# A cross-attention pipeline: where three key chunks are scaled, transposed and evicted

## Chip, core and metric

The kernel runs on one core of a Trainium2 chip. The metric is the time of one execution on the device, in microseconds (us), of which the median of several runs is taken. The engines are named as in the profile: PE is TensorE's matmul stream and PEld its weight loads, DVE is VectorE, ACT is ScalarE, POOL is GpSimd, SP is SyncE, which issues most DMAs.

## What is computed

A decoder layer on x of 16 batches x 100 tokens x 512, in three parts: causal self-attention with 16 heads, cross-attention to a context of 361 tokens per batch, and a feed-forward layer that routes each token to 2 of 8 experts; a layer norm follows each. The change lies in the cross-attention, which has 16 query heads of 128 and 4 key/value heads, so that four query heads share one key head:

```python
q = (hidden_states @ Wq + bq).reshape(b, s, NH, HD).transpose(0, 2, 1, 3)
k = (encoder_hidden_states @ Wk + bk).reshape(b, se, NKV, HD).transpose(0, 2, 1, 3)
v = (encoder_hidden_states @ Wv + bv).reshape(b, se, NKV, HD).transpose(0, 2, 1, 3)
k = jnp.repeat(k, GROUPS, axis=1)
v = jnp.repeat(v, GROUPS, axis=1)
q = _rmsnorm(q, qn_w)
k = _rmsnorm(k, kn_w)
scores = jnp.einsum('bhsd,bhed->bhse', q, k) * scale
scores = scores + attention_mask[:, None, :, :]
probs = jax.nn.softmax(scores.astype(jnp.float32), axis=-1).astype(q.dtype)
out = jnp.einsum('bhse,bhed->bhsd', probs, v)
out = out.transpose(0, 2, 1, 3).reshape(b, s, NH * HD)
return out @ Wo
```

## The kernel before

Self-attention runs first and leaves the queries of the cross-attention in memory; the feed-forward part comes last. `cross_attention_phase` takes the 16 batches one after the other. Its program is written by hand, one instruction list for each engine, and semaphores join the lists: an engine runs its own list strictly in the order written. Batches 0 and 1 are written out, batches 2 to 13 are a loop of six turns with two batches in each, and batches 14 and 15 and a rest are written out again (`over_batches`).

A batch j has four quarters s = 0 to 3, one for each key head. Every product that needs more than a single reduced-precision pass is made of three matmuls, from a high and a low part of both factors (`product3`, line 70). So whatever comes out of a matmul and goes into another is evicted from its PSUM bank twice: ScalarE writes the high part ("hi"), VectorE the low part ("lo", bank minus high part).

In quarter s, TensorE makes the scores of four heads (`scores`); between them it transposes the probabilities of the quarter before (`transpose_probs`, line 855), three chunks of 121 keys, and puts output products in (`output`). Then comes the values product of the quarter before (`values_product`, nine matmuls into `o_bank`). VectorE masks each head's scores and takes their minimum (`masked`, line 1117), ScalarE exponentiates (`exponent`, line 1014), VectorE inverts the sums in two pairs (`invert_sums`, line 1123), and GpSimd multiplies the four heads by them (`normalise`, lines 1253 and 1278). The values product is evicted by ScalarE to oTh (line 1052) and by VectorE to oTl (line 1181).

The keys of the next batch j+1 are made alongside, in three chunks c of 121 context tokens. For each chunk: `keys` (the product with Wk), `key_squares` (line 1080 adds the bias and empties the bank into the tile kn; line 1085 takes the four heads' sums of squares), `key_rsqrt` on GpSimd, `key_norm` (line 1093, the scaling of kn), `transpose_keys` (line 893, four transposes), `keys_hi` on ScalarE (line 999, tile kTh) and `keys_lo` on VectorE (line 1099, tile kTl). Chunks 0 and 2 share one half of kn. `key_norm` of chunk 0 stands in quarter 2, between the two reciprocals, that of chunk 1 likewise in quarter 3, and that of chunk 2 behind `apply_norm` (line 1245, the last step of the layer norm of the batch before). Chunk 0 is transposed in quarter 2 after output products and in front of the keys of chunk 2; chunks 1 and 2 are transposed in quarter 3, both behind the values product and in front of the last two output products. Their evictions stand behind that of the values product on ScalarE and VectorE.

The first scores of a batch wait for all three chunks of kTl. The keys of chunk 2 wait until line 1080 has emptied the bank that chunk 1 used. The transposes of chunk 1 write the bank that held chunk 0's, so they wait for chunk 0's kTl, which VectorE makes at the beginning of quarter 3.

Of the kernel before, what the change touches and what calls it, by code (L numbers as in the profile page):

```python
# [654 lines left out]
def cross_attention_phase(nc, sem, head, stage, ctxT, Wo, bk, bv, mask, ident_s, router_w, router_b, route_c, expert_w, Ehl, x1_d, q_d, x2_d):  # L655
# [6 lines left out]
    with ExitStack() as ctx:  # L662
# [172 lines left out]
        def _(pe):  # L835
# [94 lines left out]
            def body(j, par):  # L930
                first, last, past = kinds(j)
                for s in range(1 if past else 4):
# [37 lines left out]
                    if s == 3:  # L970
                        output(j, 1, range(1, 2))
                    if before:
                        values_product(n - 1, (s + 3) % 4, j)
# [3 lines left out]
                    if s == 3:  # L977
                        if not last:
                            transpose_keys(j + 1, 1)
                            transpose_keys(j + 1, 2)  # L980
                        output(j, 1, range(2, XG))
# [10 lines left out]
        def _(act):  # L992
# [40 lines left out]
            def body(j, par):  # L1033
                first, last, past = kinds(j)
                for s in range(1 if past else 4):
# [10 lines left out]
                    if first:  # L1046
                        for k in range(2):
                            split_hi(KV_PIECES + 2 * s + k)
                    if before:
                        kv = (s + 3) % 4  # L1050
                        act.wait_ge(o_done, n)
                        act.activation(oTh[:, kv, :], o_bank[:, 0:XG * S], ACT.Identity,  # L1052
                                       bias=bv_s[:, kv:kv + 1]).then_inc(o_hi, 1)
# [6 lines left out]
                    if s in (2, 3) and not last:  # L1060
                        keys_hi(j + 1, s - 2, 1 - par)
                    if s == 3 and not last:
                        keys_hi(j + 1, 2, 1 - par)
                if past:
# [4 lines left out]
        def _(dve):  # L1069
# [74 lines left out]
            def body(j, par):  # L1144
                first, last, past = kinds(j)
                for s in range(1 if past else 4):
                    n, before, now = 4 * j + s, not (first and s == 0), not past
                    for h in range(3):
# [6 lines left out]
                        if before:  # L1155
                            probs_lo(n - 1, h)
                    if s == 0 and routed(j):
                        keep_logits(j - 2)
                    if now:
                        masked(j, s, 3)  # L1160
                        invert_sums(j, s, 0)
                        if s in (2, 3) and not last:
                            key_norm(j + 1, s - 2)
                        invert_sums(j, s, 2)
# [11 lines left out]
                    if s == 3 and not last:  # L1176
                        key_norm(j + 1, 2)
                    if before:
                        kv = (s + 3) % 4
# [7 lines left out]
                    if s == 3 and not last:  # L1187
                        keys_lo(j + 1, 1, 1 - par)
                        keys_lo(j + 1, 2, 1 - par)
# [809 lines left out]
```

## Time and profile before

| | |
|---|---|
| Runs | 1589.85, 1590.1 and 1595.18 us; median 1590.1 us |
| Profiled execution | 1593.47 us, its span 1591.6 us |
| Cross-attention stage in it | about 532 to 1376 us |
| Granted clock of TensorE, mean | 0.968 of full speed |
| Busy: PE, PEld, DVE, ACT, POOL | 93%, 76%, 60%, 42%, 41% of the span |

The shares are means over three different stages. What a change inside one batch is worth shows only where TensorE waits in that batch, so the rows further down come from the list of waits and from the timeline of one batch. In the timeline a row gives start, duration, engine, line, operation and tiles; brackets at its end say how long the engine had been idle before it and which instruction it waited for.

### The profile page before, as it was taken

The page shows a single profiled execution, that of the slowest core. Times are in us where ns is not written, and L with a number is a line of the kernel's source. Part 1 is how long each engine was busy: PE and PEld are TensorE (multiplying, and loading weights), DVE is VectorE, ACT ScalarE, POOL GpSimd, SP SyncE. Part 2 cuts the span into 40 slices and gives each one's busy share as a digit, 9 for nine tenths or more (in the row PEclk, how much of TensorE's full clock was granted, in tenths as well). Part 3 has the DMA queues.
Part 4 walks back from the last instruction along what each step waited for, and adds up shares of the span by engine and source line. Part 5 has one row for each costly group of instructions (what it writes and reads, how often), then busy time and mean ns, then how long its engine had stood idle before and what let it go on. Part 6 is the DMA issues. An engine that isn't in the chain of part 4 may idle for free. (4 is left out here: it accounts for less than half of the span.)

```text
span 1591.6 us, 27704 instructions
## 1 busy us (share of the span) xinstructions
PE 1474.6 (93%) x8462; PEld 1206.2 (76%) x8462; DVE 949.7 (60%) x3585; ACT 662.4 (42%) x1789; POOL 648.4 (41%) x1000
## 2 busy tenths in 40 slices
PE   6999999999988689999999999999999999489967
PEld 6777877877866478888888888888888887367744
DVE  3666666666666565566655665566555665653457
ACT  4434334334343253444444444444444445343346
POOL 1324324324334364444444444344444443373164
PEclk8999999999999989999999999999999999789988
DMA  6221121121132332121111112111121213375373
GB/s 208 93 85 63 72 91 64 72 86 69 67 117 89 122 112 71 56 59 58 43 60 55 62 36 69 56 59 55 42 61 55 64 37 117 142 207 174 125 235 102
DMA packets 60669, 139.62 MB, mean 88 GB/s; under 512 B 10150, under 2 KB 20746, under 8 KB 59588
## 3 DMA queue, kind: packets, MB, share of 16 engines
q1 hardware_dynamic: 56008, 123.72, 23.5%
q0 software_dynamic: 4576, 14.95, 3.3%
q8 instruction: 31, 0.51, 0.1%
q14 instruction: 54, 0.44, 0.1%
HBM read 94.18 MB, written 44.46 MB: 87 GB/s over the span
## 5 line engine op out<-in xcount | busy, mean ns | idle before, releaser
L1253 POOL TENSOR_TENSOR b_pcarry<-b_half 128x1 f32<-128x1 f32 x173 | 47.6, 275 | 392.1 <-DVE b_rinv L1123 354.4
L1014 ACT ACTIVATE b_probs<-b_probs,b_nmax 100x361 f32<-100x361 f32 x256 | 152.1, 594 | 79.5 <-DVE b_nmax L1117 79.1
L70 PE MATMUL bank<-b_kTh,b_q 128*100 128x362 f32 x512 | 172.4, 337 | 9.3 <-DVE b_kTl L1099 6.0
L1117 DVE CUSTOM_DVE_ANT_0 b_probs<-bank,b_mask 100x361 f32<-100x361 f32 x256 | 135.3, 529 | 52.9 <-issue 45.2
L1278 POOL TENSOR_SCALAR b_probs<-b_probs,b_rinv 100x361 f32<-100x361 f32 x256 | 163.6, 651 | 0.0
L1110 DVE TENSOR_TENSOR b_pTl<-bank,b_pTh 121x400 fp32r<-121x400 f32 x192 | 109.7, 572 | 53.1 <-ACT b_pTh L1009 53.0
L1052 ACT ACTIVATE b_oTh<-bank,b_bv 128x400 fp32r<-128x400 f32 x64 | 38.1, 595 | 233.1 <-PE bank L70 233.1
L1009 ACT ACTIVATE b_pTh<-bank 121x400 fp32r<-121x400 f32 x192 | 96.6, 504 | 85.6 <-PE bank L855 81.3
L855 PE MATMUL bank<-ident,b_probs 100*121 100x100 f32 x768 | 111.3, 268 | 6.4 <-POOL b_probs L1278 5.6
L855 PEld LDWEIGHTS bank<-ident,b_probs 100*121 100x121 f32 x768 | 108.6, 188 | 9.0 <-POOL b_probs L1278 7.1
L70 PE MATMUL bank<-b_Woh,b_oTh 128*100 128x512 f32 x256 | 111.1, 434 | 1.4 <-DVE b_oTl L1181 1.4
L70 PEld LDWEIGHTS bank<-b_kTh,b_q 128*100 128x100 f32 x512 | 85.3, 167 | 29.3 <-issue 14.0
L70 PE MATMUL bank<-a_Wqh,a_x1Th 128*100 128x512 f32 x256 | 100.7, 393 | 2.7 <-DVE a_qn L547 1.5
L70 PE MATMUL bank<-a_Wqh,a_x1Tl 128*100 128x512 f32 x256 | 101.0, 394 | 0.0
L70 PE MATMUL bank<-b_Woh,b_oTl 128*100 128x512 f32 x256 | 100.9, 394 | 0.0
L70 PE MATMUL bank<-b_Wol,b_oTh 128*100 128x512 f32 x256 | 100.9, 394 | 0.0
L70 PE MATMUL bank<-a_Wql,a_x1Th 128*100 128x512 f32 x256 | 100.6, 393 | 0.0
L1181 DVE SCALAR_TENSOR_TENSOR b_oTl<-bank,b_bv,b_oTh 128x400 fp32r<-128x400 f32 x64 | 40.5, 633 | 97.6 <-ACT b_oTh L1052 97.6
L424 ACT ACTIVATE a_probs<-a_probs,a_nmax 100x100 f32<-100x100 f32 x256 | 92.8, 367 | 4.4 <-DVE a_nmax L500 4.4
L627 POOL TENSOR_TENSOR a_probs<-a_probs,a_rinv 100x400 f32<-100x400 f32 x64 | 54.7, 855 | 93.4 <-DVE a_rinv L507 93.3
L70 PE MATMUL bank<-b_Wkh,b_ctxh 128*121 128x512 f32 x192 | 82.2, 428 | 11.3 <-DVE b_kn L1080 8.2
L70 PE MATMUL bank<-b_kTl,b_q 128*100 128x362 f32 x256 | 84.3, 329 | 0.0
(259 smaller groups left out, 3949.4 us busy)
## 6 DMA issues: line engine op xcount, KB each, us to landing
b_q<-q_d SPq DMA_DIRECT2D x64, 400.0 KB, 3.1
q_d<-a_qo SPq DMA_DIRECT2D x62, 400.0 KB, 2.4
b_ctxr<-in_ctxT SPq DMA_DIRECT2D x48, 242.0 KB, 3.9
y_d<-c_y SPq DMA_DIRECT2D x32, 256.0 KB
c_Eraw<-in_expert_w SPq DMA_DIRECT2D x10, 512.0 KB, 7.0
a_stage<-in_Wq SPq DMA_DIRECT2D x4, 1024.0 KB
stage<-in_Wo SPq DMA_DIRECT2D x8, 512.0 KB, 4.4
a_xTr<-in_xT SPq DMA_DIRECT2D x8, 400.0 KB
```

The source lines that it names most:

```text
L70: mm = eng.matmul(out, lhsT=l(c), rhs=r(c), start=first and k == 0, stop=last and k == n - 1)
L424: e = act.activation(probs[:, r, c, :], probs[:, r, c, :], ACT.Exp, scale=-1.0, bias=nmax[:, h:h + 1], accum_out=psums[:, r, c:c + 1])
L627: pool.tensor_tensor(probs[:, r], probs[:, r], rinv[:, r].unsqueeze(2).to_broadcast([S, DC, S]), ALU.mult).then_inc(pn_rdy, 1)
L855: mm = pe.transpose(t_bank[c % 2][0:KT, h * S:(h + 1) * S], probs[:, s % 2, h, c * KT:(c + 1) * KT], ident_s[0:S, 0:S])
L1009: act.activation(pTh[:, c, :], t_bank[c % 2][0:KT, 0:XG * S], ACT.Copy).then_inc(pt_hi, 1)
L1014: act.activation(p, p, ACT.Exp, scale=-1.0, bias=nmax[:, s % 2, h:h + 1], accum_out=psums[:, s % 2, h:h + 1]).then_inc(e_rdy, 1)
L1052: act.activation(oTh[:, kv, :], o_bank[:, 0:XG * S], ACT.Identity, bias=bv_s[:, kv:kv + 1]).then_inc(o_hi, 1)
L1110: dve.tensor_tensor(pTl[:, c, :], t_bank[c % 2][0:KT, 0:XG * S], pTh[:, c, :].bitcast(F32), ALU.subtract).then_inc(pt_lo, 1)
L1117: dve.tensor_tensor_reduce(out=probs[:, s % 2, h, 0:SE], in0=s_bank[h % 2][0:S, 0:SE], in1=mask_s[:], scale=-1.0, scalar=BIG, op0=ALU.add, ...
L1181: dve.scalar_tensor_tensor(out=oTl[:, kv, :], in0=o_bank[:, 0:XG * S], scalar=bv_s[:, kv:kv + 1], in1=oTh[:, kv, :].bitcast(F32), op0=ALU.add,
L1253: pool.tensor_tensor(pcarry[:, k:k + 1], half_s[:, 0:1], half_s[:, 0:1], ALU.add)
L1278: pool.tensor_scalar(p, p, rinv[:, s % 2, h:h + 1], 1.0, ALU.mult, ALU.mult).then_inc(p_rdy, 1)
```

## The change

Five groups of instructions move inside the lists of three engines, in every batch but the last (there is no next batch there). No instruction is added, removed or resized. On TensorE, the transposes of chunk 1 go in front of the values product of quarter 3. On ScalarE, kTh of chunk 1 goes in front of oTh. On VectorE, the scaling of chunk 0 goes to the middle of quarter 2, behind the second low part of the probabilities; the scaling of chunk 1 goes in front of the last masking of quarter 3; kTl of chunk 1 goes in front of oTl.

```diff
--- before.py
+++ after.py
@@ -969,6 +969,8 @@
                             keys(j + 1, 2)
                     if s == 3:
                         output(j, 1, range(1, 2))
+                        if not last:
+                            transpose_keys(j + 1, 1)
                     if before:
                         values_product(n - 1, (s + 3) % 4, j)
                     if s == 0 and now and not first:
@@ -976,7 +978,6 @@
                         values(j, 2)
                     if s == 3:
                         if not last:
-                            transpose_keys(j + 1, 1)
                             transpose_keys(j + 1, 2)
                         output(j, 1, range(2, XG))
                 if past:
@@ -1046,6 +1047,8 @@
                     if first:
                         for k in range(2):
                             split_hi(KV_PIECES + 2 * s + k)
+                    if s == 3 and not last:
+                        keys_hi(j + 1, 1, 1 - par)
                     if before:
                         kv = (s + 3) % 4
                         act.wait_ge(o_done, n)
@@ -1058,9 +1061,7 @@
                         for c in range(KC):
                             values_hi(j, c)
                     if s in (2, 3) and not last:
-                        keys_hi(j + 1, s - 2, 1 - par)
-                    if s == 3 and not last:
-                        keys_hi(j + 1, 2, 1 - par)
+                        keys_hi(j + 1, 2 * (s - 2), 1 - par)
                 if past:
                     x2_transposed(B - 1)
             over_batches(act, body)
@@ -1154,13 +1155,15 @@
                             keys_lo(j + 1, 0, 1 - par)
                         if before:
                             probs_lo(n - 1, h)
+                        if s == 2 and h == 1 and not last:
+                            key_norm(j + 1, 0)
                     if s == 0 and routed(j):
                         keep_logits(j - 2)
                     if now:
+                        if s == 3 and not last:
+                            key_norm(j + 1, 1)
                         masked(j, s, 3)
                         invert_sums(j, s, 0)
-                        if s in (2, 3) and not last:
-                            key_norm(j + 1, s - 2)
                         invert_sums(j, s, 2)
                     if first:
                         for k in range(2):
@@ -1175,6 +1178,7 @@
                         apply_norm(j - 1)
                     if s == 3 and not last:
                         key_norm(j + 1, 2)
+                        keys_lo(j + 1, 1, 1 - par)
                     if before:
                         kv = (s + 3) % 4
                         dve.wait_ge(o_hi, n)
@@ -1185,7 +1189,6 @@
                         values_lo(j, 0)
                         values_lo(j, 1)
                     if s == 3 and not last:
-                        keys_lo(j + 1, 1, 1 - par)
                         keys_lo(j + 1, 2, 1 - par)
                     if s == 3 and not first:
                         dve.wait_ge(x2_out, 16 * j)
```

The order of the instructions at the places that matter, as the two programs have it in batch 1. VectorE, quarter 2, before (`b_pTl` is the low part of the probabilities, line 1117 the masking, 1123 the reciprocals, 1093 the scaling):

```order
L1110 TENSOR_TENSOR b_pTl<-bank,b_pTh 121x400
L1116 MEMSET b_carry 100x1
L1117 ISA b_probs,b_nmax<-bank,b_mask 100x361
L1117 ISA b_nmax 100x1
L1123 RECIPROCAL b_rinv<-b_psums 100x2
L1093 TENSOR_TENSOR b_kn<-b_kn,b_krs 121x512
L1123 RECIPROCAL b_rinv<-b_psums 100x2
L1080 TENSOR_TENSOR b_kn<-bank,b_bk 121x512
```

And now (all lines of VectorE's list are one to three numbers higher):

```order
L1111 TENSOR_TENSOR b_pTl<-bank,b_pTh 121x400
L1094 TENSOR_TENSOR b_kn<-b_kn,b_krs 121x512
L1117 MEMSET b_carry 100x1
L1118 ISA b_probs,b_nmax<-bank,b_mask 100x361
L1118 ISA b_nmax 100x1
L1111 TENSOR_TENSOR b_pTl<-bank,b_pTh 121x400
L1117 MEMSET b_carry 100x1
L1118 ISA b_probs,b_nmax<-bank,b_mask 100x361
L1118 ISA b_nmax 100x1
L1124 RECIPROCAL b_rinv<-b_psums 100x2 x2
L1081 TENSOR_TENSOR b_kn<-bank,b_bk 121x512
```

The scaling has left the place between the reciprocals and stands two maskings earlier. VectorE, end of quarter 3, before (1245 is the layer norm's last step, 1181 is oTl, 1099 is kTl):

```order
L1116 MEMSET b_carry 100x1
L1117 ISA b_probs,b_nmax<-bank,b_mask 100x361
L1117 ISA b_nmax 100x1
L1123 RECIPROCAL b_rinv<-b_psums 100x2
L1093 TENSOR_TENSOR b_kn<-b_kn,b_krs 121x512
L1123 RECIPROCAL b_rinv<-b_psums 100x2
L1245 TENSOR_SCALAR b_y<-b_y,b_mv,b_rstd 100x512
L1093 TENSOR_TENSOR b_kn<-b_kn,b_krs 121x512
L1181 SCALAR_TENSOR_TENSOR b_oTl<-bank,b_bv,b_oTh 128x400
L1099 TENSOR_TENSOR b_kTl<-bank,b_kTh 128x4x121 x2
```

And now:

```order
L1094 TENSOR_TENSOR b_kn<-b_kn,b_krs 121x512
L1117 MEMSET b_carry 100x1
L1118 ISA b_probs,b_nmax<-bank,b_mask 100x361
L1118 ISA b_nmax 100x1
L1124 RECIPROCAL b_rinv<-b_psums 100x2 x2
L1248 TENSOR_SCALAR b_y<-b_y,b_mv,b_rstd 100x512
L1094 TENSOR_TENSOR b_kn<-b_kn,b_krs 121x512
L1100 TENSOR_TENSOR b_kTl<-bank,b_kTh 128x4x121
L1185 SCALAR_TENSOR_TENSOR b_oTl<-bank,b_bv,b_oTh 128x400
L1100 TENSOR_TENSOR b_kTl<-bank,b_kTh 128x4x121
```

The first scaling stands in front of the masking, and one kTl stands in front of oTl. TensorE, end of quarter 3, before (`b_pTh,b_Vh` and its like are the values product, `ident,b_kn` the transposes):

```order
L70 MATMUL bank<-b_pTh,b_Vl 128x400
L893 MATMUL bank<-ident,b_kn 128x121 x8
L70 MATMUL bank<-b_Woh,b_oTh 100x512
```

And now:

```order
L70 MATMUL bank<-b_Woh,b_oTl 100x512
L893 MATMUL bank<-ident,b_kn 128x121 x4
L70 MATMUL bank<-b_pTh,b_Vh 128x400
L70 MATMUL bank<-b_pTl,b_Vh 128x400
L70 MATMUL bank<-b_pTh,b_Vl 128x400
L70 MATMUL bank<-b_pTh,b_Vh 128x400
L70 MATMUL bank<-b_pTl,b_Vh 128x400
L70 MATMUL bank<-b_pTh,b_Vl 128x400
L70 MATMUL bank<-b_pTh,b_Vh 128x400
L70 MATMUL bank<-b_pTl,b_Vh 128x400
L70 MATMUL bank<-b_pTh,b_Vl 128x400
L893 MATMUL bank<-ident,b_kn 128x121 x4
```

Four of the eight transposes stand in front of the nine matmuls of the values product.

## Rows read from the trace of the kernel before

**Rows 1.** The page: busy us (share of the span) and instructions of each engine.

```profile
PE 1474.6 (93%) x8462; PEld 1206.2 (76%) x8462; DVE 949.7 (60%) x3585; ACT 662.4 (42%) x1789; POOL 648.4 (41%) x1000
```

**Rows 2.** Waits of PE and PEld, 535:1380: waiter <- releaser: us, times, longest.

```profile
PE bank L70 <- DVE b_kn L1080: 8.2, 15, 3.5
...
PE bank L70 <- DVE b_kTl L1099: 6.0, 13, 1.7
...
PE bank L70 <- issue: 0.7, 2, 0.3
...
PEld bank L893 <- DVE b_kn L1093: 13.3, 17, 5.6
```

**Rows 3.** In order of time, end of batch 7: start us, duration us, engine, instruction.

```profile
951.63 0.53 DVE L1117 CUSTOM_DVE_ANT_0 b_probs<-bank,b_mask 100x361 f32<-100x361 f32 x1
...
952.80 0.34 PE L70 MATMUL bank<-b_pTh,b_Vh 121*128 121x400 f32 x1
...
953.03 0.69 DVE L1245 TENSOR_SCALAR b_y<-b_y,b_mv,b_rstd 100x512 f32<-100x512 f32 x1
...
953.64 0.67 DVE L1093 TENSOR_TENSOR b_kn<-b_kn,b_krs 121x512 f32<-121x512 f32 x1
...
954.43 0.99 PE L893 MATMUL bank<-ident,b_kn 121*128 121x121 f32 x8
...
954.63 0.59 ACT L1052 ACTIVATE b_oTh<-bank,b_bv 128x400 fp32r<-128x400 f32 x1 [1.73 <-PE bank L70]
...
955.18 0.47 PE L70 MATMUL bank<-b_Woh,b_oTh 128*100 128x512 f32 x1
...
955.25 0.63 DVE L1181 SCALAR_TENSOR_TENSOR b_oTl<-bank,b_bv,b_oTh 128x400 fp32r<-128x400 f32 x1 [0.94 <-ACT b_oTh L1052]
...
955.49 0.39 PE L70 MATMUL bank<-b_Wol,b_oTh 128*100 128x512 f32 x1
...
955.81 1.22 DVE L1099 TENSOR_TENSOR b_kTl<-bank,b_kTh 128x484 fp32r<-128x484 f32 x2
...
956.40 0.40 PE L70 MATMUL bank<-b_Woh,b_oTl 128*100 128x512 f32 x1
...
957.16 0.40 PE L70 MATMUL bank<-b_kTh,b_q 128*100 128x362 f32 x1 [0.36 <-DVE b_kTl L1099]
```

**Rows 4.** In order of time, quarter 0 (first row) and quarter 2 of batch 7.

```profile
914.29 0.17 DVE L1123 RECIPROCAL b_rinv<-b_psums 100x2 f32<-100x2 f32 x1 [0.68 <-ACT b_probs L1014]
...
937.16 0.57 DVE L1110 TENSOR_TENSOR b_pTl<-bank,b_pTh 121x400 fp32r<-121x400 f32 x1 [0.37 <-ACT b_pTh L1009]
...
937.83 0.53 DVE L1117 CUSTOM_DVE_ANT_0 b_probs<-bank,b_mask 100x361 f32<-100x361 f32 x1
...
939.07 0.33 PE L70 MATMUL bank<-b_kTh,b_q 128*100 128x362 f32 x1
...
939.44 0.53 DVE L1117 CUSTOM_DVE_ANT_0 b_probs<-bank,b_mask 100x361 f32<-100x361 f32 x1
...
939.97 0.68 DVE L1093 TENSOR_TENSOR b_kn<-b_kn,b_krs 121x512 f32<-121x512 f32 x1
...
940.74 0.17 DVE L1123 RECIPROCAL b_rinv<-b_psums 100x2 f32<-100x2 f32 x1
...
941.68 0.47 PE L70 MATMUL bank<-b_Wkh,b_ctxh 128*121 128x512 f32 x1 [0.34 <-DVE b_kn L1080]
```

**Rows 5.** Key squares by tile b_kn (min/median/max ns); GpSimd's two pairs, in time.

```profile
L1085 DVE CUSTOM_DVE_ANT_0 b_junk<-b_kn x192: 279/286/568, 537.1 to 1303.8; 121x128 f32<-121x128 f32 x192
...
952.87 1.88 POOL L1278 TENSOR_SCALAR b_probs<-b_probs,b_rinv 100x361 f32<-100x361 f32 x2
...
954.89 1.12 POOL L1278 TENSOR_SCALAR b_probs<-b_probs,b_rinv 100x361 f32<-100x361 f32 x2
```

**Rows 6.** In order of time: batch 0's last quarter, and VectorE's return in batch 8.

```profile
598.12 0.63 PE L893 MATMUL bank<-ident,b_kn 121*128 121x121 f32 x4 [1.88 <-DVE b_kn L1093]
...
960.63 0.06 DVE L1116 MEMSET b_carry<- 100x1 f32 x1 [3.61 <-PE bank L70]
```

## The prediction

> **What bounds the kernel now.** I read the page's busy line first: the matmul stream of TensorE (PE) is busy for 93% of the span and no other engine for more than 60% [rows 1]. So a change that adds no work and removes none is worth what it takes out of, or puts into, TensorE's idle time. The second view is the list of TensorE's waits in the cross-attention stage, 535 to 1380 us [rows 2]. Three of them repeat in every batch. Fifteen times the keys of chunk 2 wait for the bias add that empties their bank (line 1080). Thirteen times the first scores of a batch wait for the low part of the transposed keys, kTl (line 1099): once before batch 0 and at the ends of batches 1 to 12; two more such waits, 0.33 long at the ends of batches 13 and 14, stand there as "issue". Seventeen times a weight load (PEld) waits for a scaled chunk, kn (line 1093). Third, I read one batch in order of time; it is batch 7, and batches 1 to 14 show the same steps in the same places. [rows 3] is its last 5.5 us, [rows 4] its quarter 2.
>
> At the batch's end the last output product starts at 956.40 and the scores at 957.16. From 955.49 to 956.40 stand four steps from one output product to the next, 0.23 each, so the scores could start at 956.63, and **the stall is 0.53 us**. It happens at the end of each batch from 1 to 14: 14 x 0.53 = 7.4 us. In quarter 2 the keys of chunk 2 start at 941.68.
>
> **The change, part by part.** Nothing is added or removed, only moved. I follow each moved step along the clock of that batch.
>
> *The scaling of chunk 0 in quarter 2* (line 1093, 0.67 us) moves from between the two reciprocals to the place behind the second low-part subtraction. That one starts at 937.16, and VectorE (DVE) starts the next ready instruction some 0.52 later, so the scaling runs from 937.68 and the third masking, which started at 937.83, starts at 937.68 + 0.60 = 938.28. Its follower then runs from about 938.80, and the fourth masking could start at 939.33. It started at 939.44 because its scores (last product 939.07, 0.33 long) ended at 939.40, so it doesn't move. What did the scaling cost where it stood? In a quarter without it VectorE idles 0.68 us in front of the second reciprocal, for ScalarE's exponent (ACT): the row at 914.29. The scaling, from 939.97, is 0.68 long and filled just that hole; the reciprocal came at 940.74, when the exponent was there. The bias add that the keys of chunk 2 wait for comes behind that reciprocal, and stays [rows 4]. TensorE's transposes no longer wait for kn (the 0.37 of idle weight loading in [rows 2] goes, 15 of the 17), but what follows them starts at 941.68 all the same. **Worth 0 of the 15 stalls there**; the bounds are 0.1 us a batch on either side, the slack found above.
>
> *The scaling of chunk 1 in quarter 3* moves ahead of the last masking, where there is no hole. The masking moves from 951.63 to about 952.11, 0.48 later, and with it the exponent, the second reciprocal, the layer norm's last step (line 1245, 953.03 becomes 953.51) and the scaling of chunk 2 (953.64 becomes 954.12, so its end 954.31 becomes 954.79). GpSimd's (POOL) normalisation of the last quarter is later by the same, and ends near 956.5; the transposes that read it come behind the next scores, after 957.5. The store of x2, and the q and context loads queued behind it on SyncE, go out 0.5 us later; their readers come in the next batch's second quarter and later, and no DMA ends a wait of TensorE in the view of [rows 2]. All of that is covered.
>
> *The transposes of chunk 1* go in front of the values product, where kn is ready at 952.2 and TensorE gets there at 952.80, no wait. Eight transposes held TensorE from 954.43 to 955.26 (the next product starts at 955.18 and its successor at 955.49, 0.23 behind 955.26), so four take 0.41. The values product ends 0.41 later, and ScalarE's eviction of it starts at 955.04 where it was 954.63.
>
> *The evictions.* Before, the chain from there was: oTh 954.63, oTl 955.25, then both kTl steps from 955.81, 0.57 each, the second ending at 957.03, and the scores 0.13 later. Now only chunk 2 is left behind oTl, since chunk 1's pair stands in front. The chain is oTh 955.04, oTl 955.66, the one kTl at 955.66 + 0.57 = 956.23, its end 956.88, the scores 957.01. What goes is one step of 0.57 and what comes is 0.41: **0.15 us a batch**, not 0.53, if nothing else is late. TensorE itself would be ready at 956.63 plus its wait for chunk 2's scaling.
>
> That wait decides how much of the 0.15 is kept. Without a wait the transposes of chunk 2 start at 952.80 + 0.41 + 1.63 = 954.84, and their kn is ready at 954.79: no slack at all. What comes behind is 0.1 to start, 0.57 for four transposes, 0.05 and 0.57 for kTh, 0.04: kTl can start 1.33 after the scaling ends. The old start, 956.38, is reached when the scaling ends at 955.05. So **a delay of 0.26 us eats the gain**, and anything beyond is a loss.
>
> Such a delay has a cause in the trace. A pair of GpSimd normalisations takes 1.12 us alone and 1.88 beside line 1245 and the scaling; a key square of line 1085, 0.29 at the median, took up to 0.57 [rows 5]; in batch 7 that was the one at 942.32, while GpSimd normalised. The two engines hold each other up, by 0.28 where VectorE loses. In the new order the first normalisation runs at 952.98 to 953.54 and the second follows, just as line 1245 comes up at 953.51. Its price lies between 0 and the 0.56 of one normalisation; I take the middle of what leaves no loss, 0.13, since the nearest row (0.28) has the same two engines but a shorter instruction. The gain kept is then 0.07 us a batch.
>
> The Trainium skill, "SBUF — State Buffer", section "Who interferes with whom", says that a VectorE instruction with two SBUF inputs and a GpSimd instruction that reads SBUF exclude each other for a whole instruction, the earlier one going first. The trace agrees that they hold each other up [rows 5]; the scaling at 953.64 was not stretched though GpSimd's pair is recorded from 952.87 on, so which goes first isn't settled by the record's start. By the rule taken strictly the outcome is the second rival.
>
> *Batch 0* has no margin: its chunk 2 scaling stands behind the weight splits, and TensorE waited 1.88 us for it [rows 6]. It ends some 0.48 later now: a loss of 0.5 us once.
>
> *The loop's start.* At the even batches from 4 on, where the loop has branched back, VectorE is back late: at 960.63 for batch 8, 3.6 us after the last kTl [rows 6]. That restart follows the last kTl, which is no later than before, so nothing changes.
>
> **Sum.** 14 x 0.07 = 1.0 us gained, 0.5 lost in batch 0: 0.5 us faster. The profiled execution took 1593.47 us (span 1591.6, 1.9 around it), 3.4 above the median of 1590.1. In its scale that is 1593.0, in the median's **1589.6 us**.
>
> **The rivals.** (a) *The whole stall goes*: if the scores didn't hang on oTl's place in VectorE's queue, 14 x 0.53 - 0.5 = 6.9 us, 1583.2. Against it: the chain above is back to back from 954.63 to 957.16, and the values product at its head moves back. (b) *GpSimd goes first*, the other side: the second normalisation gets the port at 953.54, line 1245 starts at 954.10 in effect, the scaling of chunk 2 ends near 955.2, 0.2 beyond the break-even of 955.05, kTl at 956.56 and the scores at 957.34. That is 0.18 a batch slower, 14 x 0.18 + 0.5 = 3.0 us, 1593.1. For it: a 0.03 us race; against it: VectorE won the same port at 953.64. (c) *The clean case*: no interference, 14 x 0.15 - 0.5 = 1.6 us, 1588.5. (d) *The keys of chunk 2 start earlier in quarter 2*: 15 x up to 0.54 = 8 us, 1582. Against it the two equal steps of 0.84. (e) *The change does nothing there*: the order on the engines does change, so this would need both ends to cancel; it lies inside the forecast.
>
> **Chances.** Forecast (0 to 0.15 gained a batch, clean case included) 0.62; GpSimd first, 0.22; the whole stall, 0.06; quarter 2 gains, 0.03; something slower than (b), such as a later restart of VectorE after the loop's branch, 0.07. A measurement of this kernel tells 0.5% (8 us) from no change, and nearly all cases lie within it; even the whole stall is 0.43%. Faster by over 0.5%: 0.04; slower: 0.04; within: 0.92. The range must hold (b), 1593.1, and most of the way to (a); the spread of the runs, 1589.85 to 1595.18, is added to neither. I take 1585 to 1593.5.
>
> **What would show it.** In the new trace: transposes of kn in two groups of four, with the first followed by the values product without a wait; eviction oTh 0.4 later; a kTl between the scaling of chunk 2 and oTl; one kTl behind oTl; TensorE's wait for kTl at the batch's end shorter by 0 to 0.15 but there 13 or 14 times; the wait for line 1080's add still there 15 times at 0.34; the weight load's wait for kn gone from quarter 2 and small in quarter 3. Wrong would be: no wait for kTl (rival a), line 1245 or the scaling stretched by 0.3 or more (b), or quarter 2 with keys of chunk 2 starting before 941.6 in that batch's clock (d).

## The result, and the profile after

The changed kernel took **1595.3 us** (median of 20 runs, 1592.89 to 1604.36) against 1591.6 us for the kernel before (median of 20, 1588.62 to 1598.10). The ratio is 1.0026, with a 95% interval of 1.0016 to 1.0036. It is slower, by 3.7 us between the medians; the forecast was half a microsecond faster, and 1595.3 lies outside its range of 1585 to 1593.5. (The prediction had only the first three runs of the kernel before, with a median of 1590.1.) The profiled execution took 1597.4 us, with a span of 1595.6 against 1591.6. The page's busy line, which answers to [rows 1], hardly moves:

```profile
PE 1475.7 (92%) x8462; PEld 1205.8 (76%) x8462; DVE 955.6 (60%) x3585; ACT 667.0 (42%) x1789; POOL 634.6 (40%) x1000
```

The work is the same and the idle time is not, so the list of TensorE's waits from 535 to 1385 us is the next view. It answers to [rows 2] (waiter <- releaser: us, times, longest):

```profile
PE bank L70 <- DVE b_kn L1081: 11.4, 15, 4.8
...
PE bank L70 <- DVE b_nmax L1118: 6.2, 7, 1.3
...
PE bank L70 <- DVE b_kTl L1100: 1.9, 2, 1.7
```

The wait for kTl fell from 6.0 us to 1.9, as if the change had done its work. Two others grew: the bias add from 8.2 to 11.4, and a wait for the masking's minimum (`b_nmax`, line 1118), from 2.6 to 6.2 us, that the prediction never named. From 600 to 1300 us that list has this row in before, and below it the one in after. The five waits are one at each even batch from 4 to 12, where the loop has branched back:

```profile
PE bank L70 <- DVE b_nmax L1117: 2.1, 5, 0.5
```

```profile
PE bank L70 <- DVE b_nmax L1118: 5.7, 5, 1.3
```

**Where the 4.0 us of span are.** I took the start of the keys of chunk 2 in each batch as a clock mark; the row at 941.68 in [rows 4] is one of these marks, and 943.28 is the same mark in after. The distances between marks, in us:

| | before | after | sum of the differences |
|---|---|---|---|
| from the first transpose to batch 0's mark | 40.17 | 41.51 | +1.34 |
| batch 0's mark to batch 1's | 55.17 | 55.51 | +0.33 |
| eight distances without a turn of the loop | 50.80 | 50.70 | -0.83 |
| five distances across a turn | 51.36 to 51.56 | 51.91 to 52.24 | +3.12 |
| the last mark to the end of the stage | 78.58 | 78.51 | -0.07 |

That is 3.9 of the 4.0 us; the parts outside the stage differ by -0.8 and +0.8. An ordinary batch gained 0.10 us, close to the 0.07 forecast. Each turn of the loop lost 0.62.

**The ordinary batch.** The end of batch 7 in order of time, in after; it answers to [rows 3]:

```profile
953.07 0.68 DVE L1094 TENSOR_TENSOR b_kn<-b_kn,b_krs 121x512 f32<-121x512 f32 x1
...
953.67 0.53 DVE L1118 CUSTOM_DVE_ANT_0 b_probs<-bank,b_mask 100x361 f32<-100x361 f32 x1
...
954.54 1.12 POOL L1281 TENSOR_SCALAR b_probs<-b_probs,b_rinv 100x361 f32<-100x361 f32 x2
...
955.08 0.86 DVE L1248 TENSOR_SCALAR b_y<-b_y,b_mv,b_rstd 100x512 f32<-100x512 f32 x1
...
955.85 0.67 DVE L1094 TENSOR_TENSOR b_kn<-b_kn,b_krs 121x512 f32<-121x512 f32 x1
955.89 0.34 PE L70 MATMUL bank<-b_pTh,b_Vh 121*128 121x400 f32 x1
...
956.58 0.63 PE L893 MATMUL bank<-ident,b_kn 121*128 121x121 f32 x4
...
957.86 0.66 DVE L1100 TENSOR_TENSOR b_kTl<-bank,b_kTh 128x484 fp32r<-128x484 f32 x1
...
958.21 0.40 PE L70 MATMUL bank<-b_Woh,b_oTl 128*100 128x512 f32 x1
...
958.66 0.40 PE L70 MATMUL bank<-b_kTh,b_q 128*100 128x362 f32 x1
```

The scores start 0.45 behind the last output product where 0.23 would be a plain step, so the stall is 0.22 instead of 0.53. Of the 0.31 gained, 0.10 is left in the length of a batch and 0.14 went in front of the second transposes: the last values product starts at 956.26, 0.18 is a step there, and the transposes come at 956.58, because the scaling of chunk 2 runs until 956.52. From the start of the last masking to the end of that scaling it is 2.68 us in [rows 3] and 2.85 here; the 0.17 more is the layer norm's step (line 1248), stretched from 0.69 to 0.86 beside GpSimd's pair.

**The loop's turn.** The same stretch goes on; SPq is SyncE's queue of DMA issues. First before, then after. The row of VectorE's return in before, to 960.63, is in [rows 6].

```profile
953.75 0.33 SPq L824 DMA_DIRECT2D x_d<-b_y  x1
954.74 0.34 SPq L781 DMA_DIRECT2D b_q<-q_d  x1
955.37 0.86 SPq L776 DMA_DIRECT2D b_ctxr<-in_ctxT  x2
```

```profile
955.96 0.33 SPq L824 DMA_DIRECT2D x_d<-b_y  x1
956.95 0.34 SPq L781 DMA_DIRECT2D b_q<-q_d  x1
957.58 0.86 SPq L776 DMA_DIRECT2D b_ctxr<-in_ctxT  x2
...
962.90 0.06 DVE L1117 MEMSET b_carry<- 100x1 f32 x1 [4.38 <-issue]
...
963.54 0.41 PE L70 MATMUL bank<-b_kTh,b_q 128*100 128x362 f32 x1 [1.09 <-DVE b_nmax L1118]
```

VectorE's last kTl ends at 957.02 before and 958.52 after, and it is back 3.61 and 4.38 later. TensorE waited 0.32 and 1.09: in both, it feels what is over 3.29. The store of x2 goes out 3.27 before the end of the last kTl in before, and 2.56 before it in after. So the store came 0.71 closer, and VectorE's pause is 0.77 longer here (0.71 on the mean of the five turns: 3.72 and 4.43). The last instruction that VectorE has in a batch is a wait for that store (`x2_out`).

The trace has one more actor. Queue 14 (kind "instruction") brings a packet of 8 KB at each turn, and VectorE starts 1.95 to 2.00 us behind the start of this packet, at all ten turns of these two traces. No view names the engine that a packet of this queue is for; that it is VectorE's code load is read from this constant distance. The DMA view, 0.2 us at a time, shows where it stands. Stretch 958.4 to 958.6 and then 958.6 to 958.8 of before (queue: packets, MB, share of 16 engines):

```profile
q1 hardware_dynamic: 42, 0.08, 101.9%
```

```profile
q1 hardware_dynamic: 29, 0.04, 52.5%
q14 instruction: 1, 0.01, 9.7%
```

And of after, 960.7 to 960.9 and 960.9 to 961.1:

```profile
q1 hardware_dynamic: 41, 0.07, 93.6%
```

```profile
q1 hardware_dynamic: 30, 0.04, 57.2%
q14 instruction: 1, 0.01, 9.7%
```

The packet comes as the q and context loads, issued right behind the store, run out. Three things can hold VectorE's return: the last kTl, the wait for the store, and a code load that stands among the loads. The experiments tell them apart.

### The profile page after: what moved, and what is told of

It reads as the page before. It is cut to its first block and busy times, and to the rows that moved or that the text cites. A ratio compares the mean times of both kernels' runs of the same rounds, so it can differ in the third digit from the quotient of the medians.

```text
span 1595.6 us, 27704 instructions
## 1 busy us (share of the span) xinstructions
PE 1475.7 (92%) x8462; PEld 1205.8 (76%) x8462; DVE 955.6 (60%) x3585; ACT 667.0 (42%) x1789; POOL 634.6 (40%) x1000
## 5 line engine op out<-in xcount | busy, mean ns | idle before, releaser
L1256 POOL TENSOR_TENSOR b_pcarry<-b_half 128x1 f32<-128x1 f32 x173 | 42.8, 248 | 402.5 <-DVE b_rinv L1124 364.5
L1281 POOL TENSOR_SCALAR b_probs<-b_probs,b_rinv 100x361 f32<-100x361 f32 x256 | 154.8, 617 | 0.0
L70 PE MATMUL bank<-b_Wkh,b_ctxh 128*121 128x512 f32 x192 | 82.0, 427 | 14.5 <-DVE b_kn L1081 11.4
```

What stands on the lines that cost most here:

```text
L70: mm = eng.matmul(out, lhsT=l(c), rhs=r(c), start=first and k == 0, stop=last and k == n - 1)
L1256: pool.tensor_tensor(pcarry[:, k:k + 1], half_s[:, 0:1], half_s[:, 0:1], ALU.add)
L1281: pool.tensor_scalar(p, p, rinv[:, s % 2, h:h + 1], 1.0, ALU.mult, ALU.mult).then_inc(p_rdy, 1)
```

## The experiments

In the expectations, written before each run, the main theory is that the wait for the store of x2 decides when VectorE comes back. The rivals are that it is the last kTl, or the loads behind the store. The table is what I read from all the traces. "Store's lead" is from the store's issue to the end of the last kTl, "packet" from that issue to the instruction packet, both at the turns; "ordinary" is a distance of marks without a turn, "five turns" the sum of the five with one.

| kernel | store's lead | packet | VectorE's pause, mean | five turns | ordinary |
|---|---|---|---|---|---|
| before | 3.28 | 5.0 | 3.72 | 257.3 | 50.80 |
| after | 2.56 | 5.0 | 4.43 | 260.4 | 50.70 |
| a_late_wait | 2.56 | 4.5 | 3.94 | 257.9 | 50.70 |
| b_late_wait | 3.28 | 5.1 | 3.82 | 257.8 | 50.80 |
| b_norm_late | 2.30 | 5.0 | 4.70 | 262.2 | 50.80 |
| a_late_loads | 2.56 | 3.0 | 2.39 | 253.3 | 50.69 |
| a_loads_only | 2.56 | 3.6 | 3.03 | 253.5 | 50.69 |
| b_late_loads | 3.28 | 3.5 | 2.22 | 253.8 | 50.80 |
| b_loads_only | 3.28 | 3.6 | 2.37 | 253.9 | 50.80 |
| scale_back | 3.30 | 5.0 | 3.73 | 257.4 | 50.80 |
| b_chunk0_early | 3.28 | 5.1 | 3.79 | 257.6 | 50.80 |
| a_chunk0_back | 2.56 | 5.4 | 4.84 | 270.3 | 50.69 |
| scale_late_loads | 3.30 | 3.6 | 2.33 | 253.8 | 50.80 |

**The wait for the store.** In `a_late_wait` (the changed kernel) and `b_late_wait` (the kernel before) the wait moves from the end of quarter 3 to the place in the next batch where x2's tile is written again:

```diff
-                    if s == 3 and not first:
-                        dve.wait_ge(x2_out, 16 * j)
...
+                    dve.wait_ge(x2_out, 16 * j)
```

> The changed kernel with one wait moved: VectorE waits for the store of x2 (x2_out) in front of the residual add that overwrites y, one quarter into the next batch, and no longer at the end of quarter 3, in front of the loop's branch. Everything is computed. Theory S (the loop's branch stands behind the store of x2, which the change sends out later): at even batches from 4 on, VectorE's idle time between the last kTl and the next masking falls from 4.2 to 4.6 us to under 3; TensorE's five waits for nmax there (0.97 to 1.29 us each) nearly vanish, some 6 us are gained on the changed kernel, and the time falls to about 3 us below the kernel before. Rival K (the restart follows the last kTl, or the loading of code beside the q and context loads): the idle time stays at 4.2 to 4.6 us and the time stays 4 us above before.

> The kernel before with the same wait moved in the same way. Everything is computed. Theory S: the restart was behind the store there too, so VectorE's idle time of 3.6 to 3.8 us at the even batches from 4 on falls under 3 and TensorE's five waits for nmax (0.32 to 0.51) go: 2 to 3 us faster than before. Rival K: no change, idle time 3.6 to 3.8 us.

`a_late_wait` took 1592.5 us, ratio 1.0002 (0.9987 to 1.0017) to the kernel before. Its turns are 2.5 us shorter than after's, of the 3.1 that were lost; the pause went from 4.43 to 3.94, not below 3 as the theory had it. `b_late_wait` took 1592.3 us, ratio 1.0004 (0.9988 to 1.0020), and its pause stayed. So in after the store's wait comes last and costs 0.49 of the 0.71 by which the pause grew, in before it does not. But neither kernel came back early with the wait gone: something else holds VectorE for 3.8 us.

**A later store, kTl left alone.** `b_norm_late` is the kernel before with the layer norm's last step behind the scaling of chunk 2:

```diff
-                    if s == 3 and not first:
-                        apply_norm(j - 1)
                     if s == 3 and not last:
                         key_norm(j + 1, 2)
+                    if s == 3 and not first:
+                        apply_norm(j - 1)
```

> The kernel before with the layer norm's last step (line 1245) behind the scaling of chunk 2 in VectorE's list, nothing else. The store of x2 goes out about 0.6 us later, while the scaling of chunk 2 ends 0.6 earlier and the last kTl stays where it was. Everything is computed. Theory S: VectorE's restart at the even batches from 4 on is 0.6 us later with the last kTl unmoved, TensorE's waits for nmax there grow from 0.4 to 1.0, and the kernel is 3 us slower than before. Rival K: restart and time unchanged, within 0.5 us.

It took 1598.8 us, ratio 1.0045 (1.0028 to 1.0063). The kTl's are where they were: the wait for line 1099 is 6.0 us in 13 times, as in [rows 2]. The wait for the minimum is not:

```profile
PE bank L70 <- DVE b_nmax L1117: 7.3, 6, 1.5
```

The store's lead fell by 0.98 and the pause grew by 0.98, where 0.6 had been expected. This is the loss of the changed kernel, larger, made with the store and the loads behind it alone; no instruction of the change is in it, and the last kTl, which stayed, can't be the cause. The five turns are 4.9 us longer, of the 6.4 between the medians.

**The loads.** The load of the queries of the next batch's second quarter, and the context loads queued behind it, are held until that batch's first scores are done. `a_loads_only` and `b_loads_only` have this one edit, `a_late_loads` and `b_late_loads` the late wait as well:

```diff
-                    load_q(4 * j + 1, 1, 16 * j)
+                    load_q(4 * j + 1, 1, 16 * j + 1)
```

> a_late_wait with the loads of the second quarter's q and of the next context chunks issued one scores product later (SyncE waits for the batch's first scores), so that no load runs when VectorE branches back. Everything is computed. Theory T without contention: VectorE's idle time at the even batches from 4 on stays at 3.8 to 4.2 us as in a_late_wait, time unchanged. Rival L: it falls to 3 us or less, TensorE's waits for nmax there vanish, and some 3 us are gained on a_late_wait.

> The kernel before with the wait for the store in the next batch and the loads one scores product later, as in a_late_loads. Everything is computed. With VectorE's restart out of the way, what is left between this kernel and a_late_loads is the change alone: 0.13 us less for TensorE at the end of 14 batches (1.9 us) against about 1.6 more in batch 0. Theory: both within 0.5 us of each other in the cross-attention stage, batches of 50.8 here and of 50.67 there, and this kernel 2 to 4 us faster than before. Rival (the change costs something in every batch besides the restart): a_late_loads is slower than this one by 2 us or more.

> The changed kernel with the loads one scores product later, and the wait for the store of x2 where it was, in front of the loop's branch. Everything is computed. Theory D (the loads are what delays both: the store's arrival and VectorE's code): idle time at the even batches from 4 on is 2.4 us as in a_late_loads and the time is the same. Rival S (the store alone would be late by its own length): idle time 3 us or more, 1 to 3 us slower than a_late_loads.

> The kernel before with the loads one scores product later and nothing else; one look. Everything is computed. Theory D: idle time 2.4 us in place of 3.6 to 3.8, no wait of TensorE for nmax at the loop's turns, and the even batches as long as the odd ones, 50.8 us. Rival: the idle time stays above 3.3.

`a_late_loads` took 1586.7 us, ratio 0.9979 (0.9967 to 0.9991); `b_late_loads` 1587.6, 0.9968 (0.9955 to 0.9980); `a_loads_only` 1589.2, 0.9979 (0.9966 to 0.9992); `b_loads_only`, one execution, 1585.8 beside a median of 1592.3. VectorE's return in batch 8 of `a_late_loads`, and the DMA view of the 0.2 us in which its instruction packet starts, 953.9 to 954.1:

```profile
955.90 0.06 DVE L1117 MEMSET b_carry<- 100x1 f32 x1 [2.38 <-issue]
```

```profile
q14 instruction: 1, 0.01, 13.6%
```

With nothing else in flight the packet comes 0.3 to 0.5 us behind the last kTl instead of the 1.6 to 1.9 of before and the 2.3 to 2.6 of after, and the turn costs TensorE nothing: in `a_late_loads` the five distances are 50.66 to 50.67, as short as the ordinary ones. The same row in `a_loads_only`, where the wait for the store still stands at the end of the batch:

```profile
956.24 0.06 DVE L1117 MEMSET b_carry<- 100x1 f32 x1 [3.02 <-PE bank L70]
```

That is 0.64 for the wait for the store, the loads being out of the way. The releaser named, PE, had long been done. In its expectation the rival's pause came (3 us or more), but not its loss: the ratio is that of `a_late_loads`, since 3.03 is still less than the 3.29 that TensorE covers.

With the wait in place the packet comes 3.6 us behind the store's issue without the loads and 5.0 with them; the pause is that, less the store's lead, plus 1.96. With 5.0 it gives 3.68, 4.40 and 4.66 for before, after and `b_norm_late` (measured 3.72, 4.43, 4.70), with 3.6 it gives 3.00 for `a_loads_only` (3.03). The three parts of that sum are read from the same traces; what it shows is that the 5.0 stays while the lead goes from 3.28 to 2.30. It doesn't say whether the wait or the loads are last. In before it isn't the wait alone: `b_late_wait` has none there and still 5.1. The loads are issued at a fixed distance behind the store, so a later store makes them later too, against the last kTl.

The pair with late wait and late loads has the turns out of the way, and what is left between them is the change. It had been expected to be worth nothing in all, within 0.5 us. An ordinary batch of `a_late_loads` is 0.11 shorter, but its batch 0 is longer by 1.1 and the stretch in front of it by 1.3; from the first transpose to the last mark it takes 1.0 us more than `b_late_loads`, in one trace of each. The intervals of the two ratios overlap. So even without the loss at the turns these runs show no gain from the change as it stands.

**Which part of the change makes the store late.** `scale_back` is the changed kernel with both scalings back between the reciprocals, only the transposes and evictions moved. `a_chunk0_back` puts back the scaling of chunk 0 alone. `b_chunk0_early` is the kernel before with that scaling alone moved. Their edits, in this order:

```diff
-                        if s == 2 and h == 1 and not last:
-                            key_norm(j + 1, 0)
-                        if s == 3 and not last:
-                            key_norm(j + 1, 1)
...
+                        if s in (2, 3) and not last:
+                            key_norm(j + 1, s - 2)
```

```diff
-                        if s == 2 and h == 1 and not last:
-                            key_norm(j + 1, 0)
...
+                        if s == 2 and not last:
+                            key_norm(j + 1, 0)
```

```diff
+                        if s == 2 and h == 1 and not last:
+                            key_norm(j + 1, 0)
...
-                        if s in (2, 3) and not last:
-                            key_norm(j + 1, s - 2)
+                        if s == 3 and not last:
+                            key_norm(j + 1, 1)
```

> The changed kernel with the scalings of chunks 0 and 1 back between the reciprocals, in the holes where VectorE waits for the exponent; the transposes and evictions of chunk 1 stay in front of the values product and oTh, oTl. So the store of x2 goes out when it did before, and the scaling of chunk 2 isn't late. Everything is computed. Theory T (two things stand in front of the loop's branch, the last kTl and the store of x2; before they came at the same time, the change made the store late): VectorE's idle time at the even batches from 4 on is 3.6 to 4.0 us as before, the wait for kTl at a batch's end is at 0.2 or less, and the kernel takes 2 to 4 us less than the changed one and 0 to 2 less than before. Rival L (the restart is late because its code load runs beside the q and context loads, whatever comes in front): idle time 4.2 us or more.

> The changed kernel with the scaling of chunk 0 back between the two reciprocals of quarter 2; the rest of the change stays. Everything is computed. Theory P (in batch 0 the scaling in mid-quarter meets GpSimd's split of the context, which holds the port they share: it took 1.34 instead of 0.67 us): batch 0 gets back 0.6 to 1.2 us, the wait for the keys' bias add in batch 0 falls from 4.8 towards 3.5 us, batches 1 to 14 keep their length within 0.02 us. Rival: chunk 0's place also matters in every batch (15 x 0.13 us, as the list of waits grew), then about 2 us are gained on the changed kernel.

> The kernel before with the scaling of chunk 0 moved to mid-quarter 2 and nothing else; one look. Everything is computed. Theory P (in batch 0 it meets GpSimd's context split on the port that both use): the wait for the keys' bias add in batch 0 grows from 3.5 to 4.8 us and the scaling there takes 1.3 instead of 0.67; batches 1 to 14 keep 50.8 and 51.4 us. Rival: every batch longer by 0.1.

`scale_back` took 1587.9 us, ratio 0.9979 (0.9967 to 0.9992): faster than the kernel before. Its turns are before's (257.4), and the loss is gone with the scalings. Its ordinary batch is before's too, 50.80: the wait for kTl fell, but the transposes of chunk 1, now first, wait for their scaling:

```profile
PE bank L70 <- DVE b_kTl L1100: 4.2, 13, 1.7
...
PEld bank L893 <- DVE b_kn L1094: 18.8, 32, 5.6
```

So the 0.10 of an ordinary batch needs chunk 1's scaling early, and so does the loss at the turns. The 0.2% by which this kernel is faster, 3.3 us, is not in these places. Batch 0 has 1.2 of it (53.94 against 55.17), and TensorE's clock is in that. TensorE's wait for the second transposes there, 1.88 in [rows 6], is 1.73, and the stretch in which it ends and the next run at full clock; in before they don't. First before, then `scale_back` (us of the stretch, busy us and instructions of PE, PEld, DVE, ACT and POOL, granted clock, DMA share, GB/s):

```profile
598.00:602.00 4.00, 3.88 (x17) 3.13 (x17) 2.20 (x6) 0.58 (x1) 0.97 (x2) 0.67 0.67 201
```

```profile
594.00:598.00 4.00, 2.88 (x17) 2.19 (x17) 2.76 (x7) 0.58 (x1) 1.79 (x2) 1.00 0.46 128
```

The same goes for `scale_late_loads` against `b_late_loads`: waits of 1.74 and 1.88, a batch 0 of 53.16 and 54.34. `b_late_loads` and two more traces of kernels with before's scalings have 54.34 where before has 55.17; there the granted clock was back at full speed sooner after the wait for the bias add. Where the other 2 us come from, one trace of each doesn't settle.

`b_chunk0_early`, one execution, took 1592.1 us beside a median of 1590.7. Batches and turns are before's. One thing is not, the first wait for the bias add and the duration of one scaling (by line: least, median, most ns):

```profile
PE bank L70 <- DVE b_kn L1080: 11.4, 15, 4.8
```

```profile
L1093 DVE TENSOR_TENSOR b_kn<-b_kn,b_krs x48: 670/673/1335, 536.1 to 1307.6; 121x512 f32<-121x512 f32 x48
```

In before the most is 687 ns. In after they are nearly the same (11.4 and 4.8 us, 1335 ns), and batch 0 in order of time shows why; first GpSimd, then VectorE, of after:

```profile
572.79 1.24 POOL L1264 TENSOR_TENSOR b_ctxl<-b_ctxr,b_ctxh 128x484 fp32r<-128x484 f32 x1
```

```profile
573.25 1.33 DVE L1094 TENSOR_TENSOR b_kn<-b_kn,b_krs 121x512 f32<-121x512 f32 x1
```

In batch 0 the moved scaling comes while GpSimd splits the context, and takes twice its time. The masking behind it is late, so is ScalarE's exponent, and with it the weight splits that stand in front of the bias add: TensorE waits 4.84 instead of 3.46. All five kernels with this scaling early have 4.8 or 4.9 there, all others 3.5. The Trainium skill, "SBUF — State Buffer", section "Who interferes with whom", has it that a VectorE instruction with two SBUF inputs and a GpSimd one that reads SBUF shut each other out, the earlier first. The trace agrees roughly: the scaling ends 0.55 behind the end of the split, where its whole own time would be 0.67.

`a_chunk0_back` took 1600.0 us (7 runs, 1592.56 to 1604.53), ratio 1.0039 (1.0017 to 1.0062). The batch 0 wait is 3.5 again and an ordinary batch is 50.69, so the chunk 0 scaling has no part in the gain. But it is no faster than after. Its turns are the worst of all, 51.89 to 55.80, in a profiled execution that is also the slowest of the seven. Two things meet there. The pause is 4.24 to 5.27, though the store's lead is after's; its instruction packet comes 5.3 to 5.9 us behind the store at four turns, at three of them just where the last packet of the loads ends. Why it comes that late, these traces don't show. And TensorE's clock falls. TensorE's wait in batch 6, and then the stretches behind it, in the columns used above:

```profile
856.96 0.41 PE L70 MATMUL bank<-b_kTh,b_q 128*100 128x362 f32 x1 [1.74 <-DVE b_nmax L1118]
```

```profile
856.00:858.00 2.00, 1.04 (x8) 0.97 (x9) 1.53 (x7) 1.06 (x4) 0.00 (x0) 1.00 0.02 4
858.00:862.00 4.00, 4.00 (x18) 3.34 (x17) 2.35 (x10) 1.96 (x7) 0.00 (x0) 0.54 0.00 0
862.00:866.00 4.00, 4.00 (x13) 3.03 (x11) 0.21 (x2) 0.69 (x2) 2.53 (x6) 0.61 0.32 102
866.00:872.00 6.00, 6.00 (x29) 5.09 (x28) 1.53 (x3) 1.68 (x3) 2.80 (x6) 1.00 0.17 41
```

A pause of 1.38 us made a distance of 52.30, which is 50.92 beside the pause. Pauses of 1.74 and 1.69 made 55.80 and 55.75, 54.06 beside the pause, and one of 1.98 made 54.53, 52.55 beside it: 1.6 to 3.1 us more, in stretches that are in part at the lower of the two clock levels (1.2 GHz). In after the longest such pause is 1.29, in `b_norm_late` 1.50, and the granted clock behind them is 1.00.

**Together.** `scale_late_loads` is `scale_back` with the late wait and the late loads.

> scale_back with both: the wait for the store moved into the next batch, and the loads one scores product later. Everything is computed. It is the version that should beat both kernels if rival L holds (4 to 6 us below before); if only theory T holds it equals scale_back within 1 us.

It took **1583.7 us** (11 runs), ratio 0.9954 (0.9935 to 0.9973): 7 us under the kernel before, and the fastest of all. Its turns are ordinary batches, 50.76 to 50.78, which gives 3.5 us. Most of the gain comes with the loads and the late wait: `b_late_loads`, which has none of the change in it, has a ratio of 0.9968. Against that kernel the batches are the same and batch 0 is shorter, 53.16 to 54.34, for the reason given under `scale_back`.

## Why the prediction was wrong

- **The loop's start: the step that failed.** It said that VectorE's restart follows the last kTl, which is no later, "so nothing changes". It cost 5 x 0.62 = 3.1 us. The restart is held by the wait for the store of x2, VectorE's last instruction of a batch, and by a code load among the loads behind that store. `b_norm_late` and `a_late_wait` show the one, the late loads the other. The row in [rows 6] named PE as the releaser of that pause; nothing in it said kTl.
- **"All of that is covered"**, of the store and the loads 0.5 us later: the same error at its origin. I looked for readers of these DMAs on TensorE. The reader that mattered was VectorE's own wait, queued in front of its loop branch. The 0.48 itself was right. Laid on TensorE's clock (the last output product in front of the values product or the transposes starts at 952.58 before and 954.16 after, 1.58 apart), the last masking came 0.46 later. With the 0.17 of stretch that is the 0.63 by which the store came later; the last kTl ended 0.08 earlier, and the two make the 0.71 by which the store's lead shrank.
- **Batch 0: a term of the wrong size.** 0.5 us was forecast, for the second transposes; the pair of traces has 1.67. The wait of [rows 6] grew by 1.00, from 1.88 to 2.88, twice what was forecast, and the larger part came where nothing was: the scaling of chunk 0 met GpSimd's context split, and the wait for the bias add grew by 1.38. `b_chunk0_early` shows that. The two waits make 2.38, more than the 1.67; behind batch 0's mark the clock is at its lower level until 585.7 in before and 585.2 in after, for 5.2 and 4.1 us, which can give some of it back. The stretch from the first transpose to the mark runs from 38.5 to 43.0 us among the traces, so the sum for batch 0 is the least certain number here.
- **The evictions: right in the mechanism.** 0.07 a batch forecast, 0.10 measured. The 0.07 was half of the 0.15, and the prediction's own chain doesn't give it: with a delay of 0.13 the scaling ends at 954.92, kTl starts 1.33 later at 956.25 instead of 956.38, and 0.13 is kept. So by its rows the sum was 14 x 0.13 - 0.5 = 1.3 us faster, and the 0.10 lies between the two. I expected the wait for kTl to be listed 13 or 14 times; it is listed twice, because the last output product is recorded as running until 0.05 us before the scores. The count of a wait said less than the start of the instruction.
- **The port: right.** 0.17 measured at line 1248, 0.13 taken, under the break-even of 0.26. Rival (b), GpSimd first by a whole instruction of 0.56, did not come, so the rule taken as strictly as the prediction took it there doesn't hold for this line: it takes 0.53 at the least, 0.69 in before's batches and 0.86 in after's. Its total of 3.0 us slower is near what was measured, for another reason.
- **Quarter 2: right.** Worth 0, outside batch 0. The keys of chunk 2 wait 0.48 instead of the 0.34 of [rows 4]: the transposes in front of them end earlier and the bias add doesn't.

A later restart behind the branch was named, with no price and a part of 0.07. From before's rows it had one: the pause of 3.61 less TensorE's wait of 0.32 leaves 3.29 of cover, all of it used up, so each 0.1 us of a later restart costs 0.5 us in all. With the 0.61 by which the prediction itself moved the layer norm's end and so the store (0.48 and 0.13), that is 3.0 us slower. The prediction also said that a measurement tells 0.5% from no change; 20 runs of each kernel told 0.26%.

## What to carry to other kernels

A wait at the end of a loop's body holds the branch as well, so ask of each such wait what releases it, and put it where the data is used. Where an engine comes back late after a branch, look at the instruction queue and at what other DMAs are in flight at that time; holding back loads that nobody needs yet gave more here than the whole reordering. When a cover is already used up in the profile of before (a wait of 0.3 that is there five times), price the case that it moves, even if no reason for it is in sight.

## What the runs showed of the hardware

- A turn of the loop keeps VectorE away for 2.2 to 2.6 us with no loads in flight and for 3.5 to 4.2 with the q and context loads, where no late store holds it. About 1.96 of it lies behind the start of one 8 KB packet (1.93 to 2.19 at all 65 turns). What fills that time isn't shown. The Trainium skill, "Advanced Engine Details and Errata", section "Control Flow Timing", gives some 108 ns for a compare-and-branch. No row here shows the branch by itself, but a turn of this loop takes twenty times that and more.
- This packet often starts just as the loads run out (in before, after, `b_norm_late` and `scale_back` at nearly all 20 turns; in before 0.04 to 0.12 MB are then still to come), but in `a_late_wait` it starts at all five turns with 0.20 to 0.29 MB still to come. Whether it queues behind them or is only slowed is not settled.
- VectorE's scaling took 1.335 us instead of 0.67 beside one GpSimd instruction.
- Behind a TensorE pause of 1.74 us in steady work (`a_chunk0_back`) the granted clock was 0.54 and 0.61 of full speed in two stretches of 4 us; behind pauses of 1.69 and 1.98 it fell too. Behind pauses of 1.38 there and of up to 1.50 in `b_norm_late` it stayed 1.00, and so it did behind the 1.73 and 1.74 in batch 0 of `scale_back` and `scale_late_loads`. So the length of the pause alone doesn't decide it.
